# One early-fusion megakernel: the LoRA combination as one float32r product per tile, and new order tables for all engines

## The chip, the cores and the metric

The kernel runs on 1 core of one Trainium2 chip. The metric is device time in microseconds (us), the median of 3 runs. The core has five engines that run their own instruction streams in order and meet at semaphores: TensorE (PE, with its weight loads PEld), VectorE (DVE), ScalarE (ACT), GpSimd (POOL), and SyncE (SP), which here only issues DMAs.

## The reference, cut to what matters

64 images go through a tokenizer (a patch convolution, attention inside 3x3 windows, a class token), are joined with 77 text tokens to 87 tokens of 256 channels each, and then through 16-head attention and a feed-forward layer with LoRA experts. The part that the arithmetic of the change touches is the last one, for each of the 64 x 87 tokens `x`:

```python
logits = x @ gate_w.T                      # 8 experts
scores = jax.nn.softmax(logits, axis=-1)
weights, idx = jax.lax.top_k(scores, 2)
base = x @ W_lin.T + b_lin
t = jnp.einsum('nd,nkdr->nkr', x, left[idx])        # rank 4
out_k = jnp.einsum('nkr,nkro->nko', t, right[idx])
lora = jnp.sum(weights[..., None] * out_k, axis=1)
return base + lora
```

The kernel computes `x @ left` for all 8 experts (32 numbers a token) in the same product as `W_lin` and the logits, weighs them (0 for the experts not taken), and multiplies the 32 weighted numbers with `right` (32 x 256).

## The kernel before

**The work.** `patch_tokens` makes the patch and class tokens in 5 steps ("windows" in the code) of 13 images. `attention_ffn` does attention and feed-forward in 16 groups of 4 images: 348 tokens, held as 3 tiles of 116. Every part of the work is a named step, and each engine has its piece of it: for attention on one image `k` of a group, PE runs `peak` (scores once in float32r, for the maximum), DVE `max`, PE `mT` and ACT `mT` (the maximum, transposed), PE `scores` (subtract it and compute the scores), ACT `exp`, PE `pv` (times the values), ACT `oT`, PE `oN`, DVE `norm`, PE `oB`, ACT `oB`, POOL `oB_lo`. For a tile, PE runs `qk`, `v`, `qkT`, later `proj`, `yT`, `ffn`, `twT` and `lora`, and ACT copies each result out of PSUM under the same name.

**PSUM.** The scores of one image fill the four banks of `p_s`. The step `peak` of an image may start only when `exp` of the image before has read them. `p_a` (one bank) serves `qk`, `v` and `qkT`; `p_c` (one bank) serves `proj`, `yT`, `ffn`, `twT` and `lora` in turn, each waiting until the one before is copied out:

```python
if name == 'peak':
    use('S', S['s_exp'], n4)
```

**What sets the order.** Each engine has two tables of steps with a time (`WINDOW_PE`, `GROUP_PE`, `GROUP_ACT`, ...). `play` adds the start of the patch step or group to each time, sorts all steps by the sum, and emits them. The times are nothing but keys of this sort: an engine runs its steps in this order and waits on semaphores inside each. Group `g+1` is written 27.6 us behind group `g`, so in the steady state one engine interleaves three groups: attention of group g, the `qk`/`v`/`qkT` steps of groups g+1 and g+2, and `proj` to `lora` of groups g-1 to g-3.

**LoRA before.** `weigh` (DVE) writes `tw`, 116 tokens x 3 tiles x 32. One transpose (`twT`, PE) turns all three tiles into 96 rows x 116 columns, ACT copies them to the stationary operand `twT` (97 rows, the last one ones), and for each tile `lora` multiplies it in plain float32 with a `right` that is zero outside the tile's 32 rows; row 97 adds the bias.

Of the kernel before, what the change touches and what calls it, by code (L numbers as in the profile page):

```python
# [85 lines left out]
class Constants:  # L86


    def __init__(self, nc, ctx):
# [42 lines left out]
    LOADS = 3 + 1 + TILES + 1  # L132

    def load_weights(self, nc, sp, io):
        sources = (io['w_qkv'][:, 0:2 * C], io['w_qkv'][:, 2 * C:3 * C], io['w_ffn'], io['w_proj'])
# [2 lines left out]
        sp.wait_ge(self.S['zeroed'], 1)
        for t in range(TILES):
            sp.dma_start(self.right[LR * t:LR * (t + 1), t], io['right']).then_inc(self.w_in, 16)  # L140
        sp.dma_start(self.right[TILES * LR:TILES * LR + 1], io['rows'][TOKEN_ROWS + 1:TOKEN_ROWS + 2].unsqueeze(1).broadcast_to(
            [1, TILES, C])).then_inc(self.w_in, 16)
# [112 lines left out]
WINDOW_DVE = table("""stats.0.-10 stats.1.48 xlo.0.55 stats.2.89 xlo.1.105 xlo.2.110 stats.3.147 xlo.3.162 xlo.4.172 stats.4.176
                stats.5.183 stats.6.224 xlo.5.231 xlo.6.257 stats.7.304 stats.8.310 red_var.0.331 xlo.7.338
                redb.0.342 xlo.8.375 q.0.380 q_kb.0.384 prod.0.400 score.0.427 prod.1.437 score.1.467 prod.2.477
                score.2.498 s_max.0.517 att.0.538 sum.0.620 sum.1.638 lo.0.695 lo_var.0.700 patch.0.730 gv.0.752
                g_m.0.774 g_att.0.818 gw.0.866 cls.0.960""")
# [1312 lines left out]
```

## Time and profile before

| what | value |
|---|---|
| runs | 741.1, 741.35, 742.57 us; median 741.35 us |
| profiled execution: first to last instruction | 734.0 us |
| PE, DVE, POOL, ACT busy | 673.9, 531.2, 491.0, 432.0 us |
| share of the span | 92%, 72%, 67%, 59% |
| mean granted TensorE clock | 0.967 |

The profiled execution's own device time is not listed; its span of 734.0 us is 7.35 us below the median of the runs, which also holds what lies around the first and last instruction. A busy time is the union of an engine's instructions. Matmuls overlap in the array, so what one costs PE is read from start to start, not from its own duration. The span has four stretches: patch steps to about 210 us, the change-over to 305 us, the steady groups to 672 us, and the end.

### The profile page before, as it was taken

Reading aid. Unit: us, or ns where it says so; the run is one execution under the profiler, and the core shown is the slowest. Engines: PE = TensorE matmul, PEld = TensorE weight load, DVE = VectorE, ACT = ScalarE, POOL = GpSimd, SP = SyncE. Lnnn points to the kernel's source line nnn. Section 1 sums busy time; section 2 is a strip of 40 time slices with the busy share of each in tenths; the row PEclk is TensorE's granted clock in tenths of the full one; section 3 lists DMA queues with packets and bytes.
Section 4 is the critical chain, followed back from the end, with each engine's and each line's share of the span. In section 5 each row is a group of like instructions: output and inputs, shape, how many; then the busy total and the mean of one; then the engine's idle time right before and its main releaser. Section 6 shows DMA issues by size and latency. Waiting matters only on the chain.

```text
span 734.0 us, 24407 instructions
## 1 busy us (share of the span) xinstructions
PE 673.9 (92%) x9431; PEld 564.8 (77%) x9431; DVE 531.2 (72%) x1192; ACT 432.0 (59%) x1115; POOL 491.0 (67%) x564
## 2 busy tenths in 40 slices
PE   5998998999985799999999999999999999999873
PEld 3987887888853577888888888888888888887652
DVE  2468687887978646788878878878878887866642
ACT  4553452635442346677777676677776777776541
POOL 3667563764648428787877877876976977975442
PEclk9999999999996969999999999999999999999996
DMA  8963472231011223223232332332332332122001
GB/s 222 237 163 116 129 224 47 54 83 44 22 24 40 59 54 79 63 70 82 67 78 73 75 83 73 79 82 72 78 83 68 79 86 67 42 54 62 26 25 34
DMA packets 69528, 58.73 MB, mean 80 GB/s; under 512 B 30607, under 2 KB 68646, under 8 KB 69286
## 3 DMA queue, kind: packets, MB, share of 16 engines
q1 hardware_dynamic: 69414, 57.18, 30.9%
q8 instruction: 76, 1.25, 0.7%
q14 instruction: 38, 0.31, 0.1%
HBM read 33.69 MB, written 11.40 MB: 61 GB/s over the span
## 4 chain that ended last, share of the span: by engine, by line
PE 71%; DVE 12%; issue 4%; ACT 4%; SPq 3%; POOL 3%; DMA 2%; POOLq 0%; DVEq 0%; ACTq 0%
PE p_a L1355 13%; PE p_c L1355 10%; PE p_conv L758 8%; PE p_kv L758 7%; PE p_o L1427 6%; PE p_s L1415 5%; PE p_mm L758 4%; PE p_s L1397 4%; PE p_n L1435 3%; PE p_c L1474 3%; PE p_a L1381 3%; PE p_s L1411 2%; DVE t L1282 2%; DMA kr<-qkT 2%; DVE kv L656 1%
## 5 line engine op out<-in xcount | busy, mean ns | idle before, releaser
L1291 DVE TENSOR_REDUCE mx<-p_s 87x16 bf16<-87x1392 f32 x64 | 102.5, 1602 | 44.6 <-PE p_s L1397 44.4
L1214 ACT ACTIVATE prT<-p_s 87x1392 f32<-87x1392 f32 x64 | 85.2, 1331 | 29.3 <-PE p_s L1415 27.8
L1121 POOL TENSOR_TENSOR t<-t,ss_rs 116x512 f32<-116x512 f32 x48 | 50.9, 1060 | 58.9 <-ACT ss_rs L1190 57.8
L426 POOL TENSOR_TENSOR xs_lo<-xcols,xs_hi 120x585 fp32r<-120x585 f32 (+1 forms) x45 | 60.4, 1348 | 43.7 <-ACT xs_hi L483 43.7
L1415 PE MATMUL p_s<-qr,kr 32*87 32x87 f32 x2048 | 68.8, 257 | 0.0
L1115 POOL TENSOR_TENSOR t<-t 116x512 f32<-116x512 f32 x48 | 62.4, 1299 | 5.6 <-DVE t L1282 5.6
L1135 POOL TENSOR_TENSOR yT_lo<-y_raw,yT_hi 128x232 fp32r<-128x232 f32 x48 | 32.5, 678 | 47.1 <-issue 31.4
L1124 POOL TENSOR_TENSOR t<-t,tabs 116x512 f32<-116x512 f32 x48 | 61.2, 1276 | 2.7
L1415 PEld LDWEIGHTS p_s<-qr,kr 32*87 32x87 f32 x2048 | 60.3, 154 | 0.0
L1411 PE MATMUL p_s<-mxT,pick_row 32*87 32x87 bf16 x1024 | 55.7, 208 | 1.9 <-ACT mxT L1208 1.9
L1427 PE MATMUL p_o<-prT,vp 87*32 87x87 f32 x2048 | 55.1, 248 | 0.1
L1427 PEld LDWEIGHTS p_o<-prT,vp 87*32 87x32 f32 x2048 | 43.9, 142 | 9.8 <-issue 3.2
L1130 POOL TENSOR_TENSOR onT_lo<-on_raw,onT_hi 128x174 fp32r<-128x174 f32 x64 | 37.0, 586 | 20.2 <-ACT onT_hi L1226 11.9
L1186 ACT ACTIVATE sq<-p_a 116x512 f32<-116x512 f32 x48 | 28.8, 600 | 36.5 <-PE p_a L1355 36.4
L440 POOL TENSOR_TENSOR red<-red,pe 117x256 f32<-117x256 f32 (+1 forms) x35 | 27.5, 785 | 31.9 <-ACT pe L491 30.9
L515 ACT COPY kv<-p_kv 117x512 f32<-117x512 f32 (+1 forms) x45 | 26.6, 590 | 30.9 <-PE p_kv L758 30.9
L1279 DVE TENSOR_TENSOR t<-p_a,tabs 116x512 f32<-116x512 f32 x48 | 32.9, 685 | 15.4 <-ACT sq L1186 15.4
L1435 PE MATMUL p_n<-ident,oT 128*87 128x128 f32 x256 | 40.2, 280 | 1.2 <-ACT onT_hi L1226 1.2
L1411 PEld LDWEIGHTS p_s<-mxT,pick_row 32*87 32x87 bf16 x1024 | 32.5, 117 | 11.5 <-issue 5.1
L1204 ACT ACTIVATE vt<-p_a,a_rs 116x256 f32<-116x256 f32 x48 | 22.6, 474 | 28.4 <-PE p_a L1355 28.4
L758 PE MATMUL p_conv<-w_conv_hi,xs_hi 120*117 120x256 f32 (+1 forms) x225 | 38.1, 299 | 0.0
L1397 PE MATMUL p_s<-kr,qr 32*87 32x88 f32 x1024 | 33.3, 256 | 4.3 <-ACT prT L1214 2.1
(287 smaller groups left out, 2077.8 us busy)
## 6 DMA issues: line engine op xcount, KB each, us to landing
xcols<-in_x_cols SPq DMA_DIRECT2D x12, 822.7 KB, 8.1
h<-h_tokens SPq DMA_DIRECT2D x16, 348.0 KB
out<-out_sb SPq DMA_DIRECT2D x48, 116.0 KB
h_tokens<-in_txt SPq DMA_DIRECT2D x4, 1232.0 KB, 8.7
x<-in_txt_cols SPq DMA_DIRECT2D x32, 154.0 KB, 4.1
qr<-qkT SPq DMA_DIRECT2D x64, 58.0 KB, 2.0
kr<-qkT SPq DMA_DIRECT2D x64, 58.0 KB, 2.0
vp<-vt SPq DMA_DIRECT2D x32, 87.0 KB
```

The lines of the kernel that those rows point to most:

```text
L426: nc.gpsimd.tensor_tensor(xs.lo[:, n % XS_SLOTS, :, 0:M].bitcast(F32R), raw, xs.hi[:, n % XS_SLOTS, :, 0:M], ALU.subtract).then_inc(S['xs_ ...
L758: mm_ = nc.tensor.matmul(out, a, b, start=(c == 0), stop=(c == len(lhs) - 1))
L1115: link(nc.gpsimd.tensor_tensor(t1[:, b], t1[:, b], t2[:, b], ALU.add))
L1124: nc.gpsimd.tensor_tensor(by_head(t1[:, b]), by_head(t1[:, b]), table(2, k), ALU.add).then_inc(S['rope_ok'], 1)
L1214: nc.scalar.activation(prT[:, k % 2], p_s[0:SEQ, :, 0:QUADS * SEQ], ACT.Exp, scale=HD ** -0.5).then_inc(S['s_exp'], 1)
L1291: nc.vector.reduce_max(mx[:, k % 2, :, 0:QUADS], p_s[0:SEQ, :, 0:QUADS * SP].rearrange("p j (a k) -> p j a k", k=SP)[:, :, :, 0:SEQ], AX_X ...
L1355: mm_ = nc.tensor.matmul(out, a, b, start=(c == 0), stop=(c == len(lhs) - 1))
L1397: mm_ = nc.tensor.matmul(p_s[0:SEQ, j, a * SP:(a + 1) * SP], rows(qr, j, a, SEQ).bitcast(F32R), rows(kr, j, a, SP).bitcast(F32R), start=Tr ...
L1411: nc.tensor.matmul(p_s[0:SEQ, j, a * SEQ:(a + 1) * SEQ], pick_row[ROW * j:ROW * (j + 1), a], mxT[ROW * j:ROW * (j + 1), k % 2], start=True ...
L1415: mm_ = nc.tensor.matmul(p_s[0:SEQ, j, a * SEQ:(a + 1) * SEQ], rows(kr, j, a, SEQ), rows(qr, j, a, SEQ), start=False, stop=True, skip_grou ...
L1427: mm_ = nc.tensor.matmul(p_o[ROW * j:ROW * (j + 1), a * SEQ:(a + 1) * SEQ], vp[:, half, k, :, 4 * a + j], prT[:, k % 2, j, a * SEQ:(a + 1) ...
L1435: mm_ = nc.tensor.transpose(p_n[0:SEQ, c * P:(c + 1) * P], oT[:, k % 2, c], ident[:])
```

## The change

**LoRA.** `tw` gets three copies of the 32 weighted numbers for each tile (three DVE instructions in place of one). Three transposes give a 96 x 348 block. ACT copies it rounded to float32r; a new DVE step `tw_lo` subtracts the rounded part in rows 32 to 63, so that `twT` holds high, low and high parts over a `right_3` of high, high and low parts. One float32r product per tile then gives high x high + low x high + high x low and the bias. The operands `right_3` and `right_hi` are made once, on ACT in `rstd_a` and on POOL in `hb` of group 0; a fill of `right` at the start and a wait of SP for it go away.

**Order.** All ten tables are replaced, and the starts of the 5 patch steps and 16 groups are written out one by one (`WINDOW_AT`, `GROUP_AT`) in place of a period. A few buffers are declared in another place.

```diff
 def play(windows, window_step, groups, group_step):
-    turns = [(WINDOW_PERIOD * s + time, window_step, name, s, k) for s in range(STEPS) for name, k, time in windows]
-    turns += [(GROUP_START + GROUP_PERIOD * g + time, group_step, name, g, k) for g in range(GROUPS) for name, k, time in groups]
+    turns = [(WINDOW_AT[s] + time, window_step, name, s, k) for s in range(STEPS) for name, k, time in windows]
+    turns += [(GROUP_AT[g] + time, group_step, name, g, k) for g in range(GROUPS) for name, k, time in groups]
...
-GROUP_PERIOD, GROUP_START = 276, 2100
+GROUP_AT = (212164, 239679, 267170, 294783, 322234, 349680, 377175, 404685, 432227, 459744, 487351, 514850, 542305,
+            569802, 597394, 624987)
...
                             nc.gpsimd.tensor_tensor(w.lo[:].bitcast(F32R), raw[:], w.hi[:], ALU.subtract).then_inc(S['w2_low'], 1)
+                        pool.wait_ge(S['w2_low'], 2)
+                        pool.wait_ge(W['cls_ok'], STEPS)
+                        ready(nc.gpsimd.memset(twT[3 * LR:LORA_K], 1.0))
+                        pool.wait_ge(S['w2_high'], 3)
+                        lows = slice(2 * LR, LORA_K)
+                        ready(nc.gpsimd.tensor_tensor(right_3[lows].bitcast(F32R), right[lows], right_hi[lows], ALU.subtract))
+                        bias = slice(3 * LR, 3 * LR + 1)
+                        nc.gpsimd.tensor_copy(right_3[bias].bitcast(F32R), right_hi[bias]).then_inc(S['w2_low'], 1)
+                        pool.wait_ge(S['w2_low'], 3)
...
+                        nc.scalar.copy(right_3[0:2 * LR].bitcast(F32R), right[0:2 * LR])
+                        nc.scalar.copy(right_hi[:].bitcast(F32R), right[:]).then_inc(S['w2_high'], 1)
...
-                    nc.scalar.copy(twT[0:TILES * LR], product('gate', g, k)[0:TILES * LR, 0:TP]).then_inc(S['twT_out'], 1)
+                    nc.scalar.copy(twT[0:3 * LR].bitcast(F32R), product('gate', g, k)[0:3 * LR, 0:GT].rearrange("p (t n) -> p t n", t=TILES)
+                                   ).then_inc(S['twT_out'], 1)
...
+                    for tile in range(TILES):
+                        last = nc.vector.tensor_tensor(
+                            tw[:, tile].rearrange("p (n e r) -> p n e r", n=3, r=RANK),
+                            f[:, half, tile, C:C + LR].rearrange("p (e r) -> p e r", r=RANK).unsqueeze(1).broadcast_to(shape),
+                            g_w[:, tile].unsqueeze(1).unsqueeze(3).broadcast_to(shape), ALU.mult)
+                    last.then_inc(S['tw_ok'], 1)
+                if name == 'tw_lo':
+                    dve.wait_ge(S['twT_out'], g + 1)
+                    lows = slice(LR, 2 * LR)
+                    nc.vector.tensor_tensor(twT[lows].bitcast(F32R), product('gate', g, k)[lows, 0:GT].rearrange("p (t n) -> p t n", t=TILES),
+                                            twT[lows], ALU.subtract).then_inc(S['tw_low'], 1)
...
-                    nc.tensor.transpose(product('gate', g, k)[0:TILES * LR, 0:TP], tw[:].rearrange("p t n -> p (t n)"),
-                                        ident[0:TP, 0:TP]).then_inc(S['twT_ok'], 1)
+                    for tile in range(TILES):
+                        mm_ = nc.tensor.transpose(product('gate', g, k)[0:3 * LR, TP * tile:TP * (tile + 1)],
+                                                  tw[:, tile], ident[0:TP, 0:TP])
+                    mm_.then_inc(S['twT_ok'], 1)
...
-                    pe.wait_ge(S['twT_out'], g + 1)
+                    pe.wait_ge(S['tw_low'], g + 1)
                     for n, tile in enumerate(LORA_TILES[k]):
-                        mm_ = nc.tensor.matmul(product('lora', g, k)[0:TP, n * C:(n + 1) * C], twT[:], right[:, tile], start=True, stop=True)
+                        mm_ = nc.tensor.matmul(product('lora', g, k)[0:TP, n * C:(n + 1) * C], twT[:, tile].bitcast(F32R),
+                                               right_3[:].bitcast(F32R), start=True, stop=True)
```

What the tables do is seen in the rows that an engine gets. The first place is ACT in a steady group, from the copy of the transposed maximum (`mxT`) of a group's image 0 to the `exp` (`prT<-p_s`) of that image. The copies `f<-p_c` are of `ffn`, two groups back. Before:

```order
L1208 CAST mxT<-p_s 128x87
L1230 ACTIVATE c_ln<-c_mv,eps5 116x3
L1231 ACTIVATE c_rs<-c_ln 116x3
L1243 ACTIVATE f<-p_c,c_rs 116x296
L1189 ACTIVATE ss_ln<-ss,epsb 116x32
L1190 ACTIVATE ss_rs<-ss_ln 116x32
L1214 ACTIVATE prT<-p_s 87x1392
L1243 ACTIVATE f<-p_c,c_rs 116x296
```

After:

```order
L1227 CAST mxT<-p_s 128x87
L1205 ACTIVATE sq<-p_a 116x512
L1208 ACTIVATE ss_ln<-ss,epsb 116x32
L1209 ACTIVATE ss_rs<-ss_ln 116x32
L1249 ACTIVATE c_ln<-c_mv,eps5 116x3
L1250 ACTIVATE c_rs<-c_ln 116x3
L1262 ACTIVATE f<-p_c,c_rs 116x296 x2
L1233 ACTIVATE prT<-p_s 87x1392
```

`exp` of image 0 stood ahead of the copy of `ffn` tile 1, and now stands behind it. PE's order there is as it was: after `scores` of image 0 come `oB`, the six matmuls of that `ffn`, `pv`, and `peak` of image 1.

The second place is ACT around images 1 and 2 of the group, from the copy `f` of `ffn` tile 2 to `exp` of image 2 (the second `prT`). Before:

```order
L1204 ACTIVATE vt<-p_a,a_rs 116x256
L1214 ACTIVATE prT<-p_s 87x1392
L1195 COPY qkT<-p_a 128x4x116
...
L1250 ACTIVATE g_e<-f,g_max 116x8 x3
L1225 COPY on_raw<-p_n 128x174
L1226 CAST onT_hi<-p_n 128x2x87
L1214 ACTIVATE prT<-p_s 87x1392
L1195 COPY qkT<-p_a 128x4x116
L1236 COPY y_raw<-p_c 128x232
L1237 CAST yT_hi<-p_c 128x232
```

After:

```order
L1262 ACTIVATE f<-p_c,c_rs 116x296
L1214 COPY qkT<-p_a 128x4x116
L1233 ACTIVATE prT<-p_s 87x1392
...
L1244 COPY on_raw<-p_n 128x174
L1245 CAST onT_hi<-p_n 128x2x87
L1214 COPY qkT<-p_a 128x4x116
L1255 COPY y_raw<-p_c 128x232
L1256 CAST yT_hi<-p_c 128x232
L1233 ACTIVATE prT<-p_s 87x1392
```

`exp` of image 1 now stands behind the copy of `qkT` tile 0 of the next group, and `exp` of image 2 behind the copies of `qkT` tile 1 and `yT` tile 0.

The third place is PE from the end of `scores` of image 2 to `peak` of image 3 (`p_s<-kr,qr`), and of `scores` of image 1 to `peak` of image 2. Before, the first of them and then the second:

```order
L1355 MATMUL p_c<-w_p_hi,onT_lo 116x256 x2
L1381 MATMUL p_a<-ident,t 128x116 x4
L1435 MATMUL p_n<-ident,oT 87x128 x4
L1455 MATMUL p_c<-ident,h 128x116 x2
L1397 MATMUL p_s<-kr,qr 87x88 x16
...
L1435 MATMUL p_n<-ident,oT 87x128 x4
L1474 MATMUL p_c<-right,twT 116x256
L1381 MATMUL p_a<-ident,t 128x116 x4
L1427 MATMUL p_o<-prT,vp 32x87 x16
L1397 MATMUL p_s<-kr,qr 87x88 x16
```

After:

```order
L1409 MATMUL p_a<-ident,t 128x116 x4
L1483 MATMUL p_c<-ident,h 128x116 x2
L1463 MATMUL p_n<-ident,oT 87x128 x4
L1425 MATMUL p_s<-kr,qr 87x88 x16
...
L1463 MATMUL p_n<-ident,oT 87x128 x4
L1504 MATMUL p_c<-right,twT 116x256
L1409 MATMUL p_a<-ident,t 128x116 x4
L1425 MATMUL p_s<-kr,qr 87x88 x16
```

The six matmuls of a `proj` tile went ahead of `scores` of image 2, and `pv` of image 0 went behind `peak` of image 2, so fewer matmuls stand between the scores of an image and the `peak` of the next.

## Rows read from the trace of the kernel before

**Rows 1.** Windows of all engines: busy us (instructions) PE, PEld, DVE, ACT, POOL; clock; DMA.

```profile
210.00:305.14 95.14, 77.33 (x1034) 59.81 (x1033) 63.59 (x134) 46.09 (x113) 60.52 (x59) 0.84 0.24 57
305.14:643.92 338.78, 335.42 (x6107) 286.38 (x6108) 275.67 (x623) 245.34 (x637) 268.73 (x324) 1.00 0.29 74
643.92:671.91 27.99, 26.87 (x504) 22.92 (x505) 19.33 (x43) 19.35 (x52) 19.79 (x24) 1.00 0.21 54
671.91:734.00 62.09, 40.85 (x577) 32.30 (x577) 26.85 (x74) 24.58 (x70) 21.78 (x35) 0.88 0.12 34
```

**Rows 2.** Timeline, scores to peak of images 0 and 1: start, us, engine, line.

```profile
507.35 0.37 PE L1441 MATMUL p_n<-ident,on 87*128 87x87 f32 x2
507.50 1.34 ACT L1214 ACTIVATE prT<-p_s 87x1392 f32<-87x1392 f32 x1
507.51 0.51 PE L1355 MATMUL p_c<-w_f_hi,yT_hi 128*116 128x296 f32 x2
508.13 0.44 PE L1355 MATMUL p_c<-w_f_hi,yT_lo 128*116 128x296 f32 x2
508.74 0.49 ACT L1243 ACTIVATE f<-p_c,c_rs 116x296 f32<-116x296 f32 x1
509.28 0.51 PE L1397 MATMUL p_s<-kr,qr 32*87 32x88 f32 x16
509.84 1.60 DVE L1291 TENSOR_REDUCE mx<-p_s 87x16 bf16<-87x1392 f32 x1 [1.63 <-PE p_s L1397]
```

**Rows 3.** Timeline, scores of image 1 to peak of image 2.

```profile
513.77 0.67 PE L1435 MATMUL p_n<-ident,oT 128*87 128x128 f32 x4
513.92 1.33 ACT L1214 ACTIVATE prT<-p_s 87x1392 f32<-87x1392 f32 x1 [0.22 <-PE p_s L1415]
514.28 0.60 PE L1474 MATMUL p_c<-right,twT 97*116 97x256 f32 x2
514.71 0.56 PE L1381 MATMUL p_a<-ident,t 116*128 116x116 f32 x4
515.21 0.85 PE L1427 MATMUL p_o<-prT,vp 87*32 87x87 f32 x32
515.31 0.56 ACT L1195 COPY qkT<-p_a 128x464 f32<-128x464 f32 x1
515.99 0.51 PE L1397 MATMUL p_s<-kr,qr 32*87 32x88 f32 x16
```

**Rows 4.** Timeline, the step yT on PE and ACT and the next peak.

```profile
493.68 0.36 PE L1455 MATMUL p_c<-ident,h 116*128 116x116 f32 x2
493.97 0.51 PE L1397 MATMUL p_s<-kr,qr 32*87 32x88 f32 x16
494.08 0.35 ACT L1236 COPY y_raw<-p_c 128x232 f32<-128x232 f32 x1
494.32 0.36 ACT L1237 CAST yT_hi<-p_c 128x232 fp32r<-128x232 f32 x1
```

**Rows 5.** Tiles twT and tw: ns min/median/max, first and last start.

```profile
L1474 PE MATMUL p_c<-right,twT x94: 377/379/747, 330.4 to 726.8; 97*116 97x256 f32 x94
L1255 ACT COPY twT<-p_c x15: 242/252/259, 329.3 to 711.3; 96x116 f32<-96x116 f32 x15
L1332 DVE TENSOR_TENSOR tw<-f,g_w x16: 257/258/619, 326.5 to 724.2; 116x96 f32<-116x96 f32 x16
```

**Rows 6.** Timeline, float32r matmuls of 256 columns (two in each row).

```profile
510.21 0.40 PE L1355 MATMUL p_a<-w_v,xT_hi 128*116 128x256 f32 x2
510.44 0.39 PE L1355 MATMUL p_a<-w_v_hi,xT_lo 128*116 128x256 f32 x2
```

**Rows 7.** Windows of PE alone: busy (instructions), granted clock, DMA share, GB/s.

```profile
224.00:228.00 4.00, 2.02 (x9) 0.59 0.03 7
700.00:704.00 4.00, 2.67 (x44) 1.00 0.02 6
```

**Rows 8.** The chain that ended last, in the change-over.

```profile
279.00 1.23 POOL w_p_lo L1145
```

More of the change, by code:

```diff
@@ L137, in load_weights @@
             sp.dma_start(w, source.rearrange("(k p) n -> p k n", p=P)).then_inc(self.w_in, 16)
[L138 to L142, printed above, removed]
+        for n in range(3):
+            sp.dma_start(self.right[LR * n:LR * (n + 1)], io['right']).then_inc(self.w_in, 16)
+        sp.dma_start(self.right[3 * LR:LORA_K], io['rows'][TOKEN_ROWS + 1].unsqueeze(0).broadcast_to([2, C])).then_inc(self.w_in, 16)
     def fill_early(self, nc, pool, link):
@@ L255 @@
[L255 to L259, printed above, removed]
@@ L913 @@
-GROUP_DVE = table("""stats.0.-202 stats.1.-176 stats.2.-169 eps.0.-130 rotate.0.-17 ss.0.43 rotate.1.58 ss.1.114 rotate.2.173
-                ss.2.201 max.0.292 max.1.361 max.2.427 max.3.499 norm.0.522 norm.1.561 norm.2.603 norm.3.688
-                h2.0.733 h2.1.749 stats_c.0.791 stats_c.1.805 h2.2.861 stats_c.2.866 logits.0.950 rank.0.996
-                weigh.0.1038 out.0.1104 out.1.1109 out.2.1248""")
-GROUP_PE = table("""qk.0.-48 qk.1.19 v.0.84 qkT.0.131 qk.2.148 qkT.1.194 v.1.211 qkT.2.277 peak.0.281 mT.0.315 scores.0.325
-                peak.1.353 mT.1.378 scores.1.388 pv.0.412 peak.2.419 mT.2.444 scores.2.453 oN.0.475 peak.3.482
-                pv.1.497 mT.3.520 pv.2.522 scores.3.529 oN.1.548 oB.0.569 oN.2.587 oB.1.611 pv.3.622 oB.2.651
-                oN.3.674 oB.3.715 proj.0.722 proj.1.739 yT.0.756 yT.1.771 proj.2.838 ffn.0.869 ffn.1.890
-                yT.2.911 ffn.2.932 twT.0.1072 lora.0.1092 lora.1.1232""")
@@ L922 @@
-GROUP_POOL = table("""xc.0.-264 xlo.0.-86 add.0.33 scale.0.63 shift.0.110 add.1.153 scale.1.166 shift.1.177 add.2.220 scale.2.249
-                shift.2.260 hb.0.571 oB_lo.0.599 hb.1.582 oB_lo.1.683 oB_lo.2.688 oB_lo.3.768 hb.2.612
-                yT_lo.0.856 yT_lo.1.880 yT_lo.2.925 base.0.931 above.0.969 base.1.1036 base.2.1070""")
-GROUP_SP = table("""cols.0.-400 rows.0.-440 place.0.210 values.0.258 place.1.291 values.1.438 store.0.1111 store.1.1115 store.2.1253""")
-GROUP_PERIOD, GROUP_START = 276, 2100
+GROUP_ACT = table("""xhi.0.-10225 sq.0.-3086 rstd_a.0.-52 sq.1.1996 rstd_r.0.2193 v.0.8014 v.1.8454 qkT.0.11584 rstd_r.1.13195
+                sq.2.13226 qkT.1.20258 v.2.20937 rstd_r.2.23582 qkT.2.26780 mT.0.28907 exp.0.32013 mT.1.35370
+                exp.1.39796 mT.2.44206 oT.0.45321 exp.2.48236 oT.1.50528 mT.3.52432 exp.3.54043 oT.2.55492
+                oB.0.55975 oB.1.60477 oT.3.61966 oB.2.62894 oB.3.74618 yT.0.75689 yT.1.76500 rstd_c.0.85094
+                ffn.0.85204 ffn.1.85685 yT.2.87530 ffn.2.92971 gate.0.99884 twT.0.108839""")
@@ new lines @@
+GROUP_DVE = table("""stats.0.-19060 stats.1.-18894 stats.2.-15638 eps.0.-12300 rotate.0.-1850 ss.0.3388 rotate.1.5359 ss.1.6324
+                rotate.2.17452 ss.2.20228 max.0.29258 max.1.35909 max.2.42538 max.3.49412 norm.0.50193
+                norm.1.56555 norm.2.60107 h2.0.70425 norm.3.70737 h2.1.73523 stats_c.0.77577 h2.2.84809
+                stats_c.1.86479 stats_c.2.87325 logits.0.93328 rank.0.98810 weigh.0.101761 tw_lo.0.107783
+                out.0.108362 out.1.109577 out.2.121795""")
@@ new lines @@
+GROUP_PE = table("""qk.0.-7760 qk.1.-1273 v.0.7079 qkT.0.10602 qk.2.11930 qkT.1.15708 v.1.18884 peak.0.24087 qkT.2.24095 mT.0.26749
+                scores.0.27813 peak.1.33164 mT.1.35388 scores.1.36752 peak.2.38981 pv.0.40435 mT.2.41307
+                scores.2.42594 oN.0.44373 peak.3.44692 pv.1.47033 mT.3.48229 pv.2.48601 scores.3.49668
+                oN.1.51449 oB.0.52998 oN.2.54746 oB.1.55613 pv.3.56929 oB.2.62719 oN.3.64789 proj.0.66714
+                proj.1.69059 oB.3.69529 yT.0.71337 yT.1.74611 proj.2.80354 ffn.0.82382 ffn.1.83383 yT.2.89267
+                ffn.2.91404 twT.0.103435 lora.0.105886 lora.1.120387""")
@@ new lines @@
+GROUP_POOL = table("""xc.0.-25417 xlo.0.-6067 add.0.3356 scale.0.7386 shift.0.9120 add.1.13564 scale.1.14633 shift.1.14798 add.2.18858
+                scale.2.24640 shift.2.26388 hb.0.55777 hb.1.58748 oB_lo.0.61273 oB_lo.1.64546 hb.2.65124
+                oB_lo.2.68484 oB_lo.3.76563 yT_lo.0.78838 yT_lo.1.83756 base.0.88867 yT_lo.2.90757 base.1.91335
+                above.0.96256 base.2.112599""")
+GROUP_SP = table("""cols.0.-59088 rows.0.-45464 values.0.14418 place.0.22274 place.1.22398 values.1.28255 store.0.106129
+                store.1.116690 store.2.120545""")
@@ L965, in attention_ffn @@
         vt = sb("vt", [TP, 2, TILES, C])
-        twT = sb("twT", [TILES * LR + 1, TP])
         wp = Split(sb("w_p_hi", [P, CC, C]), sb("w_p_lo", [P, CC, C]))
```

79 lines of the change are left out of this document (41 added, 38 removed).

## The prediction

> **What bounds the kernel now.** I read the busy times by stretch first. In the steady groups PE is busy 335.42 of 338.78 us, at a granted clock of 1.00 [rows 1]. The maximum of image 0 of group 2 starts at 305.14 and that of group 14 at 643.92, so this is 12 periods of 28.23 us, and a thirteenth takes 27.99. DVE is next with 275.67, far behind. So there PE's work in series is the time: what PE no longer does is gained in full, and every time that PE stands still is lost in full. In the change-over PE stands still for 95.14 - 77.33 = 17.8 us, and at the end for 21.2 of 62.09 [rows 1]; there chains through other engines count.
>
> Then the timeline of one period. It shows a loop that has little room: `peak` of an image, 1.60 us of `max` on DVE, `mT`, `scores`, 1.34 us of `exp` on ACT, and only then `peak` of the next image, since all four banks of the scores are read by `exp`. Before, PE has just enough other work beside `exp`. From the end of `scores` of image 0 (where `oB` starts, 507.35) to `peak` of image 1 (509.28) PE does `oB`, `ffn` and `pv`, 1.93 us, while `exp` starts at 507.50 and is over at 508.84 [rows 2]. Between images 1 and 2 it is 513.77 to 515.99, 2.22 us, against an `exp` that ends at 515.25 [rows 3]. `exp` hides, because ACT starts it 0.15 us after `scores` and does the copies of `ffn` and `qkT` behind it.
>
> **The change, part by part.**
>
> *LoRA on PE.* The product of one tile takes 0.43 us from start to start, 514.28 to 514.71 [rows 3] (two records of 379 ns that overlap, 94 of them [rows 5]). A float32r product of 256 columns takes 0.23 / 2 = 0.115 us [rows 6]. Three tiles: -0.94 us. Four transposes of 116 columns take 514.71 to 515.21, so 0.125 each [rows 3]; two more cost +0.25. Together **-0.69 us a group**, and it counts, as nothing but PE bounds.
>
> *LoRA elsewhere.* DVE gets two more instructions of 0.26 us [rows 5] and `tw_lo`. For that I go between 0.26 us for 96 elements and 1.60 for 1392 [rows 2, 5]: 0.52 for 348. The ACT copy grows from 0.25 [rows 5] towards 0.45, read between that and 1.34 for 1392 elements [rows 2]. DVE comes to 275.67 / 12 = 23.0 + 1.0 us a period, ACT to 20.7, both below the period, so this load alone costs nothing. The chain from `twT` to `lora` gets longer by about 1 us, but in both orders PE does `pv`, 0.78 us (515.21 to 515.99 [rows 3]), and all of `scores` in between, and `lora` does not wait. If DVE came late to `tw_lo`, behind it stand `rotate` and `out`, and `lora`'s wait would hold PE: 0 to 0.5 us, taken as nothing.
>
> *The order of ACT.* This decides. In the steady groups `exp` of three of four images goes behind copies whose matmuls PE only does after `scores`. An engine runs its list in order, so `exp` must wait for them. With the durations of the rows, an ACT copy starting 0.04 us after the matmuls (515.27 to 515.31 [rows 3]) and as much again before `peak`:
>
> - Image 0. `ffn` ends at 508.13 + 0.44 = 508.57 [rows 2]; copy 508.61 to 509.10; `exp` to 510.44; `peak` at 510.48 instead of 509.28. PE stands still 1.20 us.
> - Image 1. `lora` shorter by 0.31, so the `qkT` transposes end at 514.71 - 0.31 + 0.56 = 514.96; copy 515.00 to 515.56; `exp` to 516.89; `peak` at 516.93. PE is free after the transposes at 514.90, since `pv` now stands behind `peak`: 2.03 us.
> - Image 2. Counted from the end of `scores`, PE does `qkT` 0.50, `yT` 0.29 (493.68 to 493.97 [rows 4]) and `oN` 0.51 (513.77 to 514.28 [rows 3]), free at 1.30. ACT copies `qkT` from 0.60 to 1.16, then the two halves of `yT`, 0.60 (494.08 to 494.68 [rows 4]), to 1.76, then `exp` to 3.09, `peak` at 3.13: 1.83 us.
> - Image 3. Nothing stands ahead of `exp`, over at 0.15 + 1.33 = 1.48, `peak` at 1.52. But PE has only `lora` 0.23 and `oN` 0.51 in between, as the next `qkT` went behind `peak`: 0.78 us.
>
> Sum **5.84 us** that PE stands still in a period. The work moved away from these places is not lost, only done earlier or later, so the period is 28.23 - 0.69 + 5.84 = 33.4. Second-order waits come on top where ACT and DVE are now bunched (the `ffn` copy of image 0 stands behind `sq` and two pairs for `rstd`); or some comes off, because 3.36 / 12 = 0.28 us of gaps in the old period [rows 1] fall inside the waits. I take +0.3, and between -0.6 and +1.6. So **+5.45 us a group**, bounds 4.5 to 6.8. There are 13 full periods, groups 2 to 14: +70.9 us.
>
> *Ends of the steady part.* Groups 0 and 1 have fewer steps of older groups, and PE waits in them anyway, so not all of the idle time is new: +5, between 2 and 10. Group 15 keeps the wait of image 0 (1.2) and a wait of `exp` for `yT` (0.6 and its matmuls, about 1). In the last chain LoRA's longer path (0.5 for `tw`, 0.2 for the copy, 0.5 for `tw_lo`) is about paid by shorter products. Together +2.7.
>
> *Set-up of the new operands.* On POOL it comes behind the two weight subtractions in `hb`, of which the one of 512 columns, 1.23 us, is in the chain that ended last [rows 8]. A subtraction of 256 columns at half of that, a copy of one row and a small fill make some 1 us, on the chain: +1.0, between 0 and 2. `cls_ok`, for which POOL waits there, comes from a patch step that is over by then. Queued behind are `oB_lo` and the rope steps; a late one would hold `proj` and `qkT`.
>
> *Patch steps.* Their tables move single steps by one or two places; each buffer that a step now needs earlier is there by the same kind of reading, and PE stays the bound. 0, between -5 and +6.
>
> Sum: 70.9 + 5 + 2.7 + 1.0 = 79.6 on a span of 734.0. With the 7.35 us by which the median of the runs stands above the span: 734.0 + 7.35 + 79.6 = **821 us**.
>
> **The clock.** While PE is idle more, its clock may fall. In the change-over, 2.02 busy of 4 us goes with a granted clock of 0.59, but at the end 2.67 of 4 goes with 1.00 [rows 7]. In the new period PE is busy 335.42 / 12 - 0.69 = 27.3 of 33.7 us, 81%, with no idle piece over about 2 us, so the sum stays at 2.4 GHz. The Trainium skill, in TensorE: Matmul & The Clock Gate, section "A second HAM failure mode: psum-queue depth-cycling", describes a kernel that idles briefly between groups of matmuls while it cycles through PSUM, and whose clock then swings between its two levels. By that rule the waits here would cost PE's clock too, and the time would be that of the clock rival below; no row of this kernel shows it at 81% busy.
>
> **Rivals.**
>
> - *PE takes the gain (the other side).* If ACT got to `exp` in time everywhere, the period would be 28.23 - 0.69 and the time 741.35 - 16 x 0.69 = 730 us. For it: PE is the bound. Against it: the order itself. It is decided by how late `exp` starts behind `scores`: PE has 1.9 us of work there for image 0, so it could start up to 0.5 us late; here it is 1.6 us late. 5%.
> - *The clock falls again and again.* If PE ran at 1.2 GHz for a third of the 440 us of steady time, those 147 us would hold 73 us of full-speed work, for which the forecast needs 73 / 0.81 = 91: +56 on the sum, 877 us. For it: 0.59 at half busy [rows 7]. Against it: 1.00 at 2.67 of 4. 9%.
> - *The waits are partly hidden.* If order differences that I read as neutral pull `ffn` and `qkT` so far ahead that half of the 5.84 us is covered, the groups cost 13 x 2.5 and the time is about 783; if nearly all of it is, gain and waits cancel. 4% and 2%.
> - *The forecast*, waits of 4.5 to 6.8 us a group with patch steps within their bounds: 80%.
>
> **How the numbers follow.** Low end of the forecast: 13 x 4.5 = 58.5, +2, -5 for the patch steps gives 797. High end: 13 x 6.8 = 88, + 10 + 3 + 2 + 6 gives 850. The clock rival holds 9%, the two faster ones 11%; the range of 8 in 10 reaches from 795 to 855. A difference within 0.2% (about 1.5 us, what a measurement of this kernel can tell from no change) needs gain and waits to cancel, 2%. Faster: 5%. Slower: 80 + 9 + 4 = 93%.
>
> **What would show it.** The period from one group's first `max` to the next is 33 to 35 us instead of 28.2. In the waits of PE the line of `peak` waits for `exp` on ACT some 5 to 6 us a group. `exp` starts 1.6 us after `scores` for image 0, about 1.7 for images 1 and 2, and 0.15 for image 3. `lora` is one record a tile, 0.12 us from start to start, and does not wait. PE's busy share in the steady part is near 80%, its clock 1.00. I am wrong if the period stays near 27.5 (the order does not bind), if the clock in the steady part is below 0.95, or if PE waits longest for something other than `exp`.

## The result and the profile after

The changed kernel takes 842.87 us (median of 4 runs, 836.44 to 845.04) against 741.23 us for the kernel before beside it: ratio 1.136, 95% interval [1.131, 1.141]. It is slower, as forecast, inside the range and 22 us above the point. The profiled execution has a span of 840.6 us against 734.0, so 106.6 us are to be explained where the forecast had 79.6. Ratios leave out single executions that took over 1.5% longer than the fastest of their kernel (one of `exp1_ahead` took 1319.8 us), but the profiles of `even_27450` (838.8 us) and `lora_copies` (759.4 us) and the first one of `exp_ahead` (931.6 us, clock 0.64) are of such executions.

Busy time by stretch comes first; columns as in [rows 1]. The maximum of image 0 of group 2 starts at 317.20, that of group 14 at 734.12, of group 15 at 768.06. The row 389.55:421.50 is group 4 alone.

```profile
247.94:283.63 35.69, 27.55 (x426) 20.77 (x427) 17.22 (x36) 13.50 (x29) 15.78 (x15) 0.76 0.22 54
283.63:317.20 33.57, 27.93 (x477) 22.09 (x478) 18.17 (x35) 17.04 (x42) 19.11 (x25) 0.85 0.21 54
...
317.20:734.12 416.92, 355.26 (x6096) 295.72 (x6097) 306.41 (x660) 243.37 (x636) 266.06 (x323) 0.92 0.23 60
389.55:421.50 31.95, 27.24 (x509) 22.91 (x510) 25.06 (x57) 20.21 (x53) 21.40 (x27) 1.00 0.26 68
...
734.12:768.06 33.94, 29.32 (x503) 24.70 (x504) 21.23 (x47) 19.00 (x51) 21.02 (x26) 0.87 0.17 45
768.06:840.60 72.54, 47.54 (x577) 38.84 (x577) 31.27 (x85) 25.70 (x72) 21.33 (x34) 0.71 0.09 26
```

The 12 periods of groups 2 to 13 take 416.92 us where before they took 338.78 [rows 1]. PE idles 61.66 us of it, 5.14 a period, and the table of PE's waits has one row for this stretch. But PE is also busy longer, 355.26 us against 335.42, with less to do: the granted clock is 0.92, not 1.00. Group 4, at 1.00, has 27.24 us of PE work.

```profile
PE p_s L1425 <- ACT prT L1233: 61.6, 48, 1.9
```

The timeline of group 4 shows two of these waits. L1469 is `oB`, which follows on `scores` of image 0, `p_c<-w_f_hi,yT_lo` is the end of `ffn` tile 1, L1262 its copy, L1409 the `qkT` transposes, L1214 their copy, L1233 is `exp`, L1425 `peak`; the number in brackets is the idle time ahead.

```profile
394.65 0.37 PE L1469 MATMUL p_n<-ident,on 87*128 87x87 f32 x2
...
395.43 0.43 PE L1383 MATMUL p_c<-w_f_hi,yT_lo 128*116 128x296 f32 x2
395.90 0.52 ACT L1262 ACTIVATE f<-p_c,c_rs 116x296 f32<-116x296 f32 x1 [1.27 <-PE p_c L1383]
396.30 1.31 ACT L1233 ACTIVATE prT<-p_s 87x1392 f32<-87x1392 f32 x1
397.67 0.51 PE L1425 MATMUL p_s<-kr,qr 32*87 32x88 f32 x16 [1.04 <-ACT prT L1233]
...
402.80 0.56 PE L1409 MATMUL p_a<-ident,t 116*128 116x116 f32 x4
403.40 0.55 ACT L1214 COPY qkT<-p_a 128x464 f32<-128x464 f32 x1 [1.43 <-PE p_a L1409]
403.84 1.33 ACT L1233 ACTIVATE prT<-p_s 87x1392 f32<-87x1392 f32 x1
405.22 0.51 PE L1425 MATMUL p_s<-kr,qr 32*87 32x88 f32 x16 [1.86 <-ACT prT L1233]
```

`scores` of image 0 gives way to `oB` at 394.65, and `exp` starts 1.6 us later, because ACT waits for `ffn` first. An ACT record starts 0.1 us before the one ahead of it has ended (395.90 + 0.52 against 396.30).

Image 2 differs between groups. In group 4 (first three rows) `exp` comes right behind the `qkT` copy; in group 8 (the rest) both halves of the `yT` copy stand between them:

```profile
411.52 0.55 ACT L1214 COPY qkT<-p_a 128x464 f32<-128x464 f32 x1 [0.29 <-PE p_a L1409]
411.96 1.33 ACT L1233 ACTIVATE prT<-p_s 87x1392 f32<-87x1392 f32 x1
...
413.34 0.51 PE L1425 MATMUL p_s<-kr,qr 32*87 32x88 f32 x16 [1.22 <-ACT prT L1233]
...
547.90 0.55 ACT L1214 COPY qkT<-p_a 128x464 f32<-128x464 f32 x1 [0.30 <-PE p_a L1409]
548.35 0.36 ACT L1255 COPY y_raw<-p_c 128x232 f32<-128x232 f32 x1
548.59 0.37 ACT L1256 CAST yT_hi<-p_c 128x232 fp32r<-128x232 f32 x1
548.83 1.35 ACT L1233 ACTIVATE prT<-p_s 87x1392 f32<-87x1392 f32 x1
...
550.23 0.51 PE L1425 MATMUL p_s<-kr,qr 32*87 32x88 f32 x16 [1.73 <-ACT prT L1233]
```

This is a time of its own for each group at work: `exp` of group g has the key 48236 + `GROUP_AT[g]`, `yT` the key 75689 + `GROUP_AT[g-1]`, and only the gaps ahead of groups 4 and 5 (27451 and 27446) are under 27453.

The clock, in windows of 2 us (length, PE busy, granted clock, DMA share, GB/s), in group 5:

```profile
434.00:436.00 2.00, 1.31 (x19) 1.00 0.20 65
436.00:438.00 2.00, 0.82 (x19) 1.00 0.19 45
438.00:440.00 2.00, 2.00 (x10) 0.67 0.30 95
440.00:442.00 2.00, 2.00 (x35) 0.50 0.27 92
442.00:444.00 2.00, 2.00 (x57) 0.98 0.19 69
```

PE stood still 1.9 of the 4 us before 438, and then worked without a gap for some 4 us at 1.2 GHz. In windows of 0.5 us the clock is low in 17 stretches between 317 and 734 us, 15 of some 3.5 us and two of 7, which I count as 19 falls; before there is none between 273 and 672. A group without a fall has 27.2 us of PE work, one with one fall 28.7, with two 30.3, with three 31.7: some 1.5 us for each. LoRA itself does what the diff says: `tw_lo`, and then two products 0.50 us together, with no wait.

```profile
418.40 0.51 DVE L1362 TENSOR_TENSOR twT<-p_c,twT 32x348 fp32r<-32x348 f32 x1 [1.03 <-ACT twT L1274]
...
419.39 0.50 PE L1504 MATMUL p_c<-right,twT 98*116 98x256 f32 x2
```

### The profile page after: what moved, and what is told of

Same layout as the page of the kernel before. It is cut to its first block, busy times and chain, and to the rows that moved or that the text cites. A ratio compares the mean times of both kernels' runs of the same rounds, so it can differ in the third digit from the quotient of the medians.

```text
span 840.6 us, 24440 instructions
## 1 busy us (share of the span) xinstructions
PE 707.7 (84%) x9415; PEld 585.0 (70%) x9415; DVE 573.7 (68%) x1240; ACT 430.1 (51%) x1117; POOL 488.9 (58%) x565
## 4 chain that ended last, share of the span: by engine, by line
PE 59%; ACT 12%; DVE 9%; DMA 5%; issue 5%; SPq 5%; POOL 4%; ACTq 0%; POOLq 0%; DVEq 0%
PE p_a L1383 12%; ACT prT L1233 8%; PE p_c L1383 7%; PE p_conv L760 7%; PE p_kv L760 5%; PE p_s L1443 5%; PE p_o L1455 5%; DMA vp<-vt 4%; PE p_s L1425 4%; SPq L1068 3%; PE p_mm L760 2%; PE p_a L1409 2%; PE p_s L1439 2%; PE p_n L1463 2%; PE p_c L1483 1%
## 5 line engine op out<-in xcount | busy, mean ns | idle before, releaser
L1425 PE MATMUL p_s<-kr,qr 32*87 32x88 f32 x1024 | 34.6, 263 | 81.3 <-ACT prT L1233 78.5
L1233 ACT ACTIVATE prT<-p_s 87x1392 f32<-87x1392 f32 x64 | 85.1, 1329 | 24.8 <-PE p_s L1443 24.7
L428 POOL TENSOR_TENSOR xs_lo<-xcols,xs_hi 120x585 fp32r<-120x585 f32 (+1 forms) x45 | 62.3, 1390 | 55.8 <-ACT xs_hi L485 55.8
L1425 PEld LDWEIGHTS p_s<-kr,qr 32*87 32x87 f32 x1024 | 26.7, 160 | 94.8 <-ACT prT L1233 91.7
L1443 PE MATMUL p_s<-qr,kr 32*87 32x87 f32 x2048 | 71.9, 265 | 0.0
L1455 PE MATMUL p_o<-prT,vp 87*32 87x87 f32 x2048 | 64.4, 276 | 0.0
L1443 PEld LDWEIGHTS p_s<-qr,kr 32*87 32x87 f32 x2048 | 63.1, 160 | 0.0
L1455 PEld LDWEIGHTS p_o<-prT,vp 87*32 87x32 f32 x2048 | 50.9, 150 | 16.4 <-issue 15.3
L1205 ACT ACTIVATE sq<-p_a 116x512 f32<-116x512 f32 x48 | 29.0, 603 | 62.1 <-PE p_a L1383 61.9
L1167 POOL TENSOR_TENSOR h<-h,f 116x256 f32<-116x256 f32 x48 | 35.2, 733 | 42.4 <-ACT f L1262 42.4
L1214 ACT COPY qkT<-p_a 128x464 f32<-128x464 f32 x48 | 26.3, 547 | 54.3 <-PE p_a L1409 54.3
L1383 PE MATMUL p_a<-w_qk_hi,xT_hi 128*116 128x512 f32 x96 | 42.3, 530 | 4.7 <-DVE t L1302 2.5
L1463 PE MATMUL p_n<-ident,oT 128*87 128x128 f32 x256 | 42.3, 289 | 1.2 <-ACT onT_hi L1245 1.2
```

Source lines behind the costliest of these rows:

```text
L428: nc.gpsimd.tensor_tensor(xs.lo[:, n % XS_SLOTS, :, 0:M].bitcast(F32R), raw, xs.hi[:, n % XS_SLOTS, :, 0:M], ALU.subtract).then_inc(S['xs_ ...
L1233: nc.scalar.activation(prT[:, k % 2], p_s[0:SEQ, :, 0:QUADS * SEQ], ACT.Exp, scale=HD ** -0.5).then_inc(S['s_exp'], 1)
L1383: mm_ = nc.tensor.matmul(out, a, b, start=(c == 0), stop=(c == len(lhs) - 1))
L1425: mm_ = nc.tensor.matmul(p_s[0:SEQ, j, a * SP:(a + 1) * SP], rows(qr, j, a, SEQ).bitcast(F32R), rows(kr, j, a, SP).bitcast(F32R), start=Tr ...
L1443: mm_ = nc.tensor.matmul(p_s[0:SEQ, j, a * SEQ:(a + 1) * SEQ], rows(kr, j, a, SEQ), rows(qr, j, a, SEQ), start=False, stop=True, skip_grou ...
L1455: mm_ = nc.tensor.matmul(p_o[ROW * j:ROW * (j + 1), a * SEQ:(a + 1) * SEQ], vp[:, half, k, :, 4 * a + j], prT[:, k % 2, j, a * SEQ:(a + 1) ...
```

## The experiments

My theory after the traces: the order of ACT makes PE wait for `exp`, and PE's idle time then makes its clock fall; about two thirds and one third of the steady loss. The rivals: LoRA's own chain costs time; the other engines' new orders carry the loss; the falls have another cause.

**The two halves of the change.** `lora_alone` has all tables of before, with

```diff
+ ... weigh.0.103800 tw_lo.0.109000 out.0.110400 ...
```

> The LoRA change alone: all ten tables and the starts of steps and groups of the kernel before, with the new step tw_lo on DVE between the ACT copy twT and the PE step lora. Theory (the new order of ACT costs all of the time, LoRA itself saves 0.69 us of PE a group): period 27.5 us in the steady groups at clock 1.00, time 730 us (727 to 735). Rival (the longer chain tw, twT, tw_lo, lora makes PE wait, or the set-up of the new operands holds the change-over): lora waits on DVE in each group, time 741 or more.

`order_alone` is the kernel before with the new tables (without `tw_lo`) and starts.

> The new tables and starts with the LoRA code of the kernel before (no tw_lo). Theory: the loss is the order's, so PE's waits for exp are as in the changed kernel, 1.0, 1.9, 1.7 and 0.6 us for the four images, and the period is longer than there by the 0.7 us of PE work: time 843 + 11 = 854 us (845 to 865). Rival (the LoRA part costs something of its own): below 843 us.

`order_alone` takes 840.3 us, ratio 1.134 [1.124, 1.143]: the order makes the whole loss. I had expected 854. PE is busy 362.82 us in its 12 periods, 7.56 more than in the changed kernel, but idles 7.2 us less, since `lora` stands inside the waits for `exp`:

```profile
318.88:736.13 417.25, 362.82 (x6111) 300.43 (x6112) 302.43 (x624) 240.81 (x636) 265.52 (x323) 0.93 0.23 60
```

So with this order the shorter LoRA products give nothing back. `lora_alone` was a surprise: 773.81 us, ratio 1.045 [1.038, 1.052], where I expected 730. Its timeline, from ACT's copy `twT` to `lora` (DVE L1297 and L1300 are `rotate` of a later group, L1360 is `tw_lo`):

```profile
483.15 0.45 ACT L1272 CAST twT<-p_c 96x348 fp32r<-96x348 f32 x1
...
483.84 0.67 DVE L1297 TENSOR_TENSOR t<-p_a,tabs 116x512 f32<-116x512 f32 x1
484.43 0.75 DVE L1300 TENSOR_TENSOR t<-p_a,tabs 116x256 f32<-116x256 f32 x2
485.21 0.51 DVE L1360 TENSOR_TENSOR twT<-p_c,twT 32x348 fp32r<-32x348 f32 x1
...
485.87 0.74 PE L1502 MATMUL p_c<-right,twT 98*116 98x256 f32 x2 [1.47 <-DVE twT L1360]
```

`tw_lo` could have started at 483.6; behind `rotate` it starts at 485.2, and PE waits 1.3 us a group (20.6 us in all). The clock falls there too, at 485.0, and in all 11 times between 350 and 680 us. Where I put `tw_lo` made this; the changed kernel has it ahead of `rotate`. So one number was moved:

```diff
- tw_lo.0.109000
+ tw_lo.0.108500
```

> The LoRA change alone in the order of before, as in the first of these kernels, with one number changed: tw_lo stands on DVE ahead of rotate of a later group (two operations, 1.4 us) instead of behind it. There tw_lo started 1.6 us after its input was there, and lora made PE wait 1.3 us in each group, 20.6 us in all. Theory (that wait, and the falls of the clock that came with it, made the LoRA change slower than before): lora waits less than 0.3 us a group, no fall in the steady groups, period 27.5 to 27.8 us, time 733 us (728 to 740). Rival (the clock falls or a wait come from something else in the LoRA part): 760 us or more.

It takes 746.76 us, ratio 1.009 [1.006, 1.013]. No fall from 275 to 680 us, so most of the wait is gone, and with it the falls; but it is still slower than before, and not 733. The waits of PE in its 12 periods, and the stretch:

```profile
PE p_a L1407 <- DVE t L1300: 4.7, 12, 0.4
PE p_s L1431 <- DVE mx L1309: 3.0, 12, 0.4
PE p_c L1502 <- DVE twT L1360: 2.5, 11, 0.2
PE p_c L1381 <- DVE h L1322: 2.2, 12, 0.2
...
306.37:651.85 345.48, 332.54 (x6096) 281.52 (x6097) 295.12 (x659) 245.97 (x636) 269.78 (x324) 1.00 0.29 73
```

Only the last of these waits was there before. PE is busy 2.9 us less than before in the 12 periods, but idles 9.6 us more, and so the period is 28.79 us instead of 28.23. DVE has 1.6 us more work a period (295.12 against 275.67 in 12), of which `tw_lo` is 0.5 and the two more instructions for `tw` are 0.9, and it lies in front of `max` of image 3, of `lora`, and of the release of `p_a` for `qkT`. Two runs tried the cause. `lora_copies` writes `tw` by copies instead of by tiles and copies `twT` earlier on ACT:

```diff
-                    for tile in range(TILES):
+                    for n in range(3):
...
-                            tw[:, tile].rearrange("p (n e r) -> p n e r", n=3, r=RANK),
+                            tw[:, :, LR * n:LR * (n + 1)].rearrange("p t (e r) -> p t e r", r=RANK),
```

> The LoRA change in the order of before with tw_lo ahead of rotate, and two edits that shorten its chain: tw is written in three instructions of one copy each over all tiles instead of one for each tile with three copies (the one of before took 0.26 us, the three now take 1.14 us together), and on ACT the copy twT stands ahead of mT of image 3 instead of behind mT and sq. Theory (the gain of 0.69 us of PE was eaten by the longer work on DVE: 0.22 us a group at mT for max, 0.22 at lora for tw_lo, 0.39 at qkT for rotate): these three waits go, period 28.0 us, time 736 us (730 to 742). Rival (the waits stay, as DVE is as loaded as before): 745 us or more.

750.27 us, ratio 1.011 [1.005, 1.016]: a miss. The three instructions took as long as before (433 ns mean), and the waits stayed (5.8, 5.3 and 6.4 us in the whole run, against 6.1, 5.2 and 6.3 in `lora_early`). The shape of `tw` is not what costs. `tw_thrice` adds only DVE work to the kernel before:

```diff
-                    nc.vector.tensor_tensor(
-                        tw[:].rearrange("p t (e r) -> p t e r", r=RANK),
+                    for n in range(3):
+                        last = nc.vector.tensor_tensor(
+                            tw[:, n].rearrange("p t (e r) -> p t e r", r=RANK),
```

> The kernel before with the DVE instruction that writes tw done three times, twice into a part that nobody reads: the added work on DVE of the new LoRA code by itself, without anything gained on PE. Theory (with the order of before, more work on DVE ahead of max of image 3 reaches PE): the three take 1.1 us instead of 0.26, PE waits 0.2 us a group more at mT for max, period 28.4 us, time 744 us (741 to 749). Rival (DVE has room, as the prediction took it): no new wait of PE, 741 us.

748.08 us, ratio 1.006 [1.003, 1.010], against a kernel before that took 743.85 us beside it. In the whole run PE has nine more waits at `mT` for `max` than before (then 2.9 us in all):

```profile
PE p_s L1407 <- DVE mx L1291: 5.9, 12, 1.4
```

In the 12 periods, 5.7 us longer than before, these waits are 2.3 us, as forecast (0.2 a period); PE is also busy 2.6 us longer, and why is open. So DVE has too little room ahead of `max` of image 3, though it is busy only 72% of the span. That this is all of the 0.9% of `lora_early` is not shown.

**The position of exp.** `exp_ahead` is the changed kernel with

```diff
- exp.0.32013  exp.1.39796  exp.2.48236
+ exp.0.30450  exp.1.38500  exp.2.47000
```

> The changed kernel with three numbers of ACT's group table changed: exp of image 0 stands again ahead of the ffn copy of tile 1, exp of image 1 ahead of the qkT copy of tile 0, exp of image 2 ahead of the copies of qkT tile 1 and yT tile 0. Theory: PE's waits for exp shrink from 5.2 us a group to 1.2 (0 for image 0, 0.3 for images 1 and 2, 0.6 for image 3), period 28.4 us, hardly any fall of the clock in the steady groups: time 750 us (742 to 768). Rival (the copies that now come later hold PE instead, or the other engines' new orders carry much of the loss): 780 us or more.

> The same kernel as exp_ahead, for a profile at an undisturbed clock. Its three undisturbed runs took 767 us where 750 were expected. Expected now: 767 us again (762 to 772), PE's waits for exp 1.2 us a group as worked out, and the 17 us either in a wait that was not seen (theory: PE for tw_lo, h or the qkT copies, 0.5 us a group or more) or in falls of the clock in the steady groups (rival: six or more of them).

768.37 us, and again 765.4 us, ratio 1.033 [1.028, 1.039]; the second profile is read. Three numbers take back 77 of 102 us. PE's groups in its 12 periods:

```profile
311.99:664.89 352.90, 328.12 (x6096) 275.02 (x6097) 304.75 (x659) 242.64 (x636) 266.24 (x324) 1.00 0.27 71
...
L1463 PE MATMUL p_n<-ident,oT 128*87 128x128 f32 x192 | 31.1, 284 | 13.3 <-ACT onT_hi L1245 13.3
L1425 PE MATMUL p_s<-kr,qr 32*87 32x88 f32 x768 | 24.5, 253 | 11.5 <-ACT prT L1233 10.8 <-DMA kr<-qkT 0.7
```

No fall of the clock. The waits for `exp` are 0.9 us a group (1.2 expected), and `oN` has a new one for ACT's copy `oB`, 1.1 us a group: the wait that I had not seen. `exp1_ahead` moves only `exp` of image 1:

> The changed kernel with one number changed: on ACT exp of image 1 stands again ahead of the qkT copy of tile 0. Theory: PE's wait ahead of peak of image 2 goes from 1.86 to 0.33 us, the others stay, 16 groups by 1.5 = 24 us, and some falls of the clock go too: time 812 us (800 to 820). Rival (the qkT copy that is now 1.3 us later holds qr and kr or the next step on PE): a new wait of 1 us or more a group and a time above 830 us.

802.82 us, ratio 1.083 [1.077, 1.089]. The waits for `exp` go from 78.5 to 55.8 us, close to the 24 expected. In the 12 periods the time falls by 39.0 us: PE idles 18.3 us less and is busy 20.7 us less, with 5 falls of the clock instead of 19. `act_old` puts back ACT's whole group table:

> The changed kernel with the whole ACT table for groups of the kernel before, all other tables and starts new. With three exp moved PE still waited for exp 1.0 us a group (images 1 to 3) and 1.1 us a group at oN for the copy oB of ACT. Theory (the wait at oN comes from ACT's new order, the rest of the waits for exp from PE's new order): the wait at oN goes, that for exp stays at 1.0 to 1.2 us, period 28.4 us, time 755 us (748 to 763). Rival (the wait at oN comes from PE's own order): 765 us or more.

780.34 us, ratio 1.054 [1.048, 1.060]: a miss by 25 us. The wait at `oN` goes, but PE now waits 20.5 us in all at `mT` for `max` of image 3, with 6 falls. Tables of different orders do not fit each other, and so this run says nothing on ACT alone.

```profile
PE p_s L1433 <- DVE mx L1311: 20.5, 16, 1.5
PE p_s L1425 <- ACT prT L1233: 13.4, 27, 1.5
```

`exp_late` does the reverse: the kernel before with

```diff
- exp.0.338  exp.1.401  exp.2.466
+ exp.0.353  exp.1.416  exp.2.487
```

> The kernel before with three numbers of ACT's group table changed, so that exp of image 0 stands behind the ffn copy of tile 1, exp of image 1 behind the qkT copy of tile 0 and exp of image 2 behind the copies of qkT tile 1 and yT tile 0, as in the changed kernel; everything else is as before. Theory (these three places make most of the loss, by waits and by the falls of the clock that the waits bring): PE waits for exp 1.1, 1.2 and 2.0 us ahead of peak of images 1, 2 and 3, period 32.4 us without a fall, 1.5 us more with one, falls in most groups: time 820 us (800 to 840). Rival (the loss needs the new orders of the other engines too): below 780 us.

825.51 us, ratio 1.114 [1.107, 1.120]. PE ahead of `peak` of images 1, 2, 3, within 0.13 us of what was expected:

```profile
520.55 0.51 PE L1397 MATMUL p_s<-kr,qr 32*87 32x88 f32 x16 [1.03 <-ACT prT L1214]
528.41 0.51 PE L1397 MATMUL p_s<-kr,qr 32*87 32x88 f32 x16 [1.07 <-ACT prT L1214]
...
536.83 0.51 PE L1397 MATMUL p_s<-kr,qr 32*87 32x88 f32 x16 [1.92 <-ACT prT L1214]
```

Undone or done alone, these three places make the larger part of the loss.

**A time of its own for each group.** `even_27450` has `GROUP_AT` = 212164 + 27450 g.

> The changed kernel with the 16 starts of groups replaced by even ones, 27.45 apart, so that exp of image 2 stands ahead of the copy of yT tile 0 in every group and not only in two. Theory: the wait ahead of peak of image 3 is 1.22 us in all groups instead of 1.73 in most, 12 x 0.5 = 6 us, with the falls of the clock as they are: time 837 us (825 to 843). Rival (a time of its own for each group does nothing): 843 us.

828.93 us, ratio 1.115 [1.109, 1.121]. The waits for `exp` fall from 78.5 to 72.5 us, the 6 expected, and another 8 us came off the median that I had not expected. The profile shows fewer falls (17 between 250 and 700 us against 26) and a new wait of 8.5 us for the `yT` copy, but it is of an execution of 838.8 us, only 3.5 us below the profiled one of the changed kernel, so it does not say where the 8 us come from. The starts are not neutral where two keys lie as close as these two, 2 to 160 apart.

**The clock.** `filled` is the changed kernel with PE kept busy in three of the four waits; the results of the added work are not used:

```diff
+                    for n in range(FILL[k] if g > 0 else 0):        # FILL = (0, 0, 12, 9)
+                        nc.tensor.transpose(p_o[:, P * (n % 4):P * (n % 4 + 1)], ident[:], ident[:])
                     use('S', S['s_exp'], n4)
...
-                    for a in range(QUADS):
+                    for a in (*range(QUADS), *range(QUADS if k == 3 else 0)):
```

> The changed kernel with PE kept busy during its waits from group 1 on: 12 transposes of 128 columns ahead of peak of image 2, 9 ahead of peak of image 3, and pv of image 3 done twice ahead of peak of image 1 of the next group; their results are not used. The waits for exp stay, only filled. Theory (the clock falls because PE idles): no fall of the granted clock in groups 2 to 14, period 32.4 us, time 843 - 30 = 813 us (806 to 822). Rival (the falls come of something else, such as the amount of work or transfers): as many falls as before, time 840 us or more.

805.4 us, ratio 1.088 [1.081, 1.095]. More work on PE makes the kernel 37 us faster:

```profile
316.16:704.75 388.59, 361.76 (x6732) 309.28 (x6733) 306.59 (x659) 242.80 (x636) 266.57 (x324) 1.00 0.25 65
```

The clock is 1.00 in this stretch, with no fall from 290 to 771 us, and 12 periods take 388.59 us, 28.3 less than in the changed kernel. `exp` is as late as there. The waits are not all filled: PE still idles 26.8 us of the 12 periods instead of 61.7, in pieces of 0.8 us at most instead of 1.9, and that was enough. The 28.3 us are the share of the clock in the steady groups.

No version with the new LoRA or the new order beats the kernel before; the nearest is `lora_early`, 0.9% behind. The tables of the patch steps were not changed on their own, so what they do is read only from the trace.

## Why the prediction was right, and where not

The 106.6 us, from the starts of `max`: up to the first, -0.7; groups 0 and 1, 69.26 against 56.5, +12.8; groups 2 to 14, 450.86 against 366.77, +84.1; the rest, 72.54 against 62.1, +10.4. The steady part by PE, for 12 periods:

| | before | after | step of the prediction |
|---|---|---|---|
| PE busy at clock 1.00 | 335.4 | 12 x 27.24 = 326.9 | -0.71 a period; -0.69 forecast |
| added by the clock | 0 | 28.4 | 0 forecast |
| PE idle | 3.4 | 61.7 | +4.86 a period; +5.84 + 0.3 forecast |

The 27.24 us are those of group 4; `exp_ahead`, at 1.00 throughout, has 328.1 us in its 12 periods, and by that the clock added 27.1.

- *PE bounds, and LoRA saves 0.69 us of it*: right as a size. That it counts in full was right only for the sum: with the new order the saving lies inside the waits (`order_alone`).
- *LoRA elsewhere costs nothing*: right for this order, where `lora` waits only at the end (2.3 us). As a rule it failed: with the order of before the new work on DVE costs more than PE gains (`lora_early`, `tw_thrice`). The sizes of `tw_lo` (0.51) and of the copy (0.46) were right, the load of DVE was not: +1.0 us a period was forecast, and it was +1.6 in `lora_early` and +2.6 in the changed kernel (306.41 against 275.67 in 12), of which the new order alone makes 2.2 (302.43 in `order_alone`). In this order nothing waited for it; the last section says what it is. The rival "PE takes the gain, 730 us" was priced too well: even with `exp` in time the LoRA change gives 747.
- *The order of ACT decides*: right, place by place. The waits are 1.03, 1.86, 1.73 and 0.59 us against 1.20, 2.03, 1.83 and 0.78 forecast. What was mis-sized for images 0 to 2 is that ACT's records were laid end to end: they overlap by 0.1 us. For image 3 `peak` came at 1.53 us, as forecast (1.52), but PE had 0.94 us of `lora` and `oN` instead of 0.74. The +0.3 for second-order waits was nothing, as PE waits for nothing else there, and the old gaps of 0.28 a period went into the waits, the lower case of the bounds. That groups 4 and 5 have another order for image 2 was not seen.
- *The clock stays at 2.4 GHz*: this step failed. The prediction itself named a steady clock below 0.95 as what would make it wrong; it is 0.92. I compared a mean busy share of 81% with a row of 2.67 busy of 4 us at 1.00 [rows 7], but that row stands once at the end, and 9 us behind it the same trace has a fall, which the forecast left out (rows below). The 28.4 us of 12 periods are 1.5 us for each of the 19 falls. The Trainium skill, TensorE: Matmul & The Clock Gate, "A second HAM failure mode: psum-queue depth-cycling", had said that brief idling between groups of matmuls costs the clock; the runs agree with it (0.92 with the waits, 1.00 with them half filled). The forecast's own rival of the clock, 877 us, took a third of the time at 1.2 GHz; it was about a sixth.
- *Groups 0 and 1, +5*: +12.8, outside its bounds. PE idles 7.9 us more than before there and is busy 4.9 us longer, at 0.80. Four more falls than before (by the same 1.5 us, 6 us) are about the difference to the forecast. *Group 15 and the end, +2.7*: +10.4. PE's waits for `tw` and `tw_lo` there (below) are 9.4 us, and were 4.0, 1.0 and 0.9 for `tw` and `twT` before: 3.5 of it. Over the whole end PE idles 3.8 us more and is busy 6.7 us longer (47.54 against 40.85) at a clock of 0.71 against 0.88 [rows 1]; how much of that lies on the last chain was not tested.

The kernel before, windows of PE alone (columns as in [rows 7]):

```profile
708.00:712.00 4.00, 2.29 (x16) 1.00 0.10 30
712.00:716.00 4.00, 3.48 (x16) 0.61 0.13 35
```

The changed kernel, PE's waits for `tw` and `tw_lo` at the end:

```profile
PE p_a L1495 <- DVE tw L1354: 4.5, 1, 4.5
...
PE p_c L1495 <- DVE tw L1354: 2.6, 1, 2.6
PE p_c L1504 <- DVE twT L1362: 2.3, 2, 1.2
```

- *Set-up on POOL +1.0, patch steps 0*: the first `max` is 0.7 us earlier than before; nothing of it shows.

So the mechanism, PE waiting for a late `exp`, was right, and that the sum came so near was in part luck: two errors partly cancel, waits 1.3 us a group too large, and the clock, left out, worth 28 us in the steady part and more at both ends. The range held because 6.8 us a group was its bound; the true 450.86 / 13 - 28.21 = 6.5 a group was reached in another way.

## What to carry to other kernels

When an in-order engine's list moves a step behind another, ask what that other step waits for, and work out each place from the timeline; that gave four waits to 0.2 us. Then ask of the bound engine not only how long it will idle but what its clock does: here short waits of 0.6 to 1.9 us, four in 34 us, cost half as much again. And an engine that is busy 72% of the span can have no slack where a chain runs through it: work added there must be held against the waits right behind it, not against the share.
